# Scaling gathered rows on ScalarE and one 18-row product for the masked maximum in a four-layer graph network on one core

## The chip, the core and the metric

One NeuronCore of a Trainium2 chip runs the whole program. It has TensorE (PE, with its weight loads listed as PEld), VectorE (DVE), ScalarE (ACT), GpSimd (POOL) and SyncE (SP), each with its own in-order instruction queue, joined by semaphores. The metric is the device time of one execution in microseconds, as the median of several runs.

## What is computed

Four graph layers over 6,250 nodes and 106,250 edges with 128 features; each adds its result to x. Only layer 0 is touched. It is a hypergraph attention layer applied twice (l = 0, 1):

```
xt = x @ W;  et = he_attr @ W
a = leaky_relu(xt[row] @ att[:H] + et[col] @ att[H:], 0.2)
amax = segment_max(a, col);  ex = exp(a - amax[col]);  den = segment_sum(ex, col)
eout = segment_sum((Binv[col] * w * ex / den[col])[:, None] * xt[row], col)
nout = segment_sum((Dinv[row] * w * ex / den[col])[:, None] * eout[col], row)
x = tanh(layernorm(nout + bias) + x)
```

The other three layers are an edge perceptron with a segment sum, a gated message layer, and two graph attentions with four heads.

## The kernel before, in words

The kernel sorts the edges twice (by destination and by source, into blocks of 128 nodes), and then makes eight passes over the sorted edges, `ORDER = "abafcdee"`. A pass handles 512 edge slots, four tiles of 128, at a time; that is a group, and a pass of layer 0 has 232. Layer 0 has four passes. The first and third are of kind `a` (by destination: masked running maximum, exponentials, sum into the destination blocks). The second is `b` and the fourth `f` (by source: the same attention weights read back, and the sum into the source blocks).

For each group POOL issues four indirect DMAs (`rows_po`, line 615) that gather 128 rows of 132 floats of the node table. DVE compares slot numbers with an iota and so makes one-hot tiles (`aOH`, `bOH`, 128x512). PE transposes them, spreads per-node numbers to edge slots with them (L883, L942), and sums the scaled rows with them (L868, L921: four fp32 products of 128x130 or 128x129 columns). The maximum in `a` is made so: ACT turns the one-hot into 0 or -1e30 (L833), adds each row's score to it (L839, four times), PE transposes that (L876), and DVE reduces along the row (L740). The gathered rows are scaled by their weight in one DVE operation of 128x512 (L799 in `a`, L974 in `b`, L1061 in `f`), which writes `aR` or `bR`, the moving operand of the sum.

All loops are software pipelines written out by hand: `sweep` calls `body(j)` on every engine, and inside it `turn(j, u, lag)` picks the group j - lag. What an engine does in iteration j is in the order of the text, and a wait holds back everything behind it on that engine. So two things count: the lag of each step and its place inside the iteration. In `b`, `b_pe(j)` does the sum of group j-5 first, then the bit product L668 and the spread of j-2, then the transposes L934 of j-1. `b_ac(j)` copies the transposed one-hot of j-1 (L1007), takes the exponential of j-3 (L1012) and copies the bits of j-2 (L672). In `f`, `f_pe(j)` does the bit product of j-2, the transposes of j-1, the sum of j-4 and the spread of j-1. The gathered tile ring `aG` has 8 entries, `bG` 4: POOL may start the gathers of group g when semaphore `S.r` says that the rows of g-8 (in `b` and `f` g-4) are scaled. `l0_ve` builds the table of a layer before its `a` pass, 13 items of four blocks, and `meet` is a barrier of all engines.

## Time and profile before

| | us |
|---|---|
| median of 3 runs | 14665.91 (14642.43 to 14757.12) |
| span of the profiled execution, first to last instruction | 11822.6 |
| difference of the two | 2843.3 |
| DVE, PE, POOL busy in the span | 8126.2, 8182.0, 7702.8 |
| layer 0: passes a, b, a, f | from 1015 to 2252, 2273 to 3508, 3604 to 4839, 4861 to 6085 |

The page of the profile gives the shares over the whole span. The passes have different limits, so they are read one by one in windows of the trace. A period below is the time that one group takes, a pass divided by 232.

### The profile page before, as it was taken

How to read it: one execution, taken by the hardware profiler on the slowest of the kernel's cores; microseconds unless marked ns; L12 is line 12 of the kernel's file. 1: busy time of each engine (PE TensorE's matmuls, PEld its weight loads, DVE VectorE, ACT ScalarE, POOL GpSimd, SP SyncE). 2: the span in 40 equal slices, each digit the busy share in tenths (PEclk: the TensorE clock that was granted, in tenths of full speed). 3: DMA queues.
4: the chain of work that ended last, by engine and by line, in shares of the span. 5: the costliest groups of instructions: out<-in, count | busy, mean ns of one | idle time of the engine just before them, and what ended most of it. 6: DMA issues, size and time to landing. Idle time of an engine off the chain costs nothing. (4 is left out here: it accounts for less than half of the span.)

```text
span 11822.6 us, 182142 instructions
## 1 busy us (share of the span) xinstructions
PE 8182.0 (69%) x47949; PEld 6566.7 (56%) x47949; DVE 8126.2 (69%) x31101; ACT 5076.1 (43%) x14757; POOL 7702.8 (65%) x7673
## 2 busy tenths in 40 slices
PE   7895777666656777555545555788886677767776
PEld 5675777544436777444434554666665444545554
DVE  9765888655556777655562222688887788878888
ACT  4553444322224444222231111466665566646665
POOL 2445777677766777677757777355653677747775
PEclk8876666655556667666567677899998666556566
DMA  1112222355542222578844444344443444434443
GB/s 17 9 20 55 53 53 53 74 130 130 128 110 60 53 53 53 134 203 205 205 131 130 132 131 128 101 145 146 147 146 100 132 134 134 133 105 134 133 134 114
DMA packets 712736, 1297.08 MB, mean 110 GB/s; under 512 B 196563, under 2 KB 369073, under 8 KB 711217
## 3 DMA queue, kind: packets, MB, share of 16 engines
q0 software_dynamic: 282368, 575.57, 22.4%
q1 hardware_dynamic: 388992, 615.05, 16.6%
q10 hardware_dynamic: 40368, 94.82, 2.1%
q8 instruction: 415, 6.80, 0.2%
q14 instruction: 593, 4.85, 0.1%
HBM read 1050.01 MB, written 234.74 MB: 109 GB/s over the span
## 5 line engine op out<-in xcount | busy, mean ns | idle before, releaser
L615 POOL DMA_INDIRECT WK<-tab,IDX x4640 | 4624.3, 997 | 1688.7 <-issue 1345.2
L1454 POOL DMA_INDIRECT B<-tab,IDX x1856 | 1774.7, 956 | 848.5 <-issue 507.3
L615 POOL DMA_INDIRECT H<-tab,IDX x928 | 878.9, 947 | 644.1 <-DVE H L1260 346.4
L1473 DVE TENSOR_REDUCE WK<-PS 128x4 f32<-128x1024 f32 x928 | 1130.4, 1219 | 190.9 <-PE PS L1599 188.6
L1584 ACT ACTIVATE B<-B 128x33 f32<-128x33 f32 x5568 | 1211.2, 308 | 8.0
L839 ACT ACTIVATE WK<-WK 128x128 f32<-128x128 f32 x1856 | 592.6, 390 | 1289.5 <-DMA WK<-tab,IDX 1265.9
L921 PE MATMUL PS<-WK 128*128 128x129 f32 x3712 | 744.2, 362 | 429.6 <-DVE WK L974 208.8
L1632 PEld LDWEIGHTS PS<-B,H 128*128 128x128 f32 x3712 | 819.8, 330 | 283.0 <-issue 274.3
L1632 PE MATMUL PS<-B,H 128*128 128x132 f32 x3712 | 880.7, 430 | 87.3 <-DVE ACC L1486 87.3
L921 PEld LDWEIGHTS PS<-WK 128*128 128x128 f32 x3712 | 638.3, 259 | 527.1 <-DVE WK L974 268.0
L921 PE MATMUL PS<-WK,B 128*128 128x129 f32 x3712 | 829.1, 394 | 12.1 <-ACT WK L1160 8.5
L1599 PE MATMUL PS<-B 27*128 27x512 bf16 x1856 | 736.8, 509 | 138.4 <-DVE WK L1473 134.3
L868 PE MATMUL PS<-B 128*128 128x130 f32 x3712 | 802.7, 385 | 1.6 <-DVE B L799 1.6
L921 PEld LDWEIGHTS PS<-WK,B 128*128 128x128 f32 x3712 | 748.9, 298 | 14.0 <-issue 13.1
L1144 DVE TENSOR_TENSOR WK<-PS,WK 128x512 f32<-128x512 f32 x232 | 160.4, 691 | 850.7 <-DMA WK<-tab,IDX 850.7
L455 POOL DMA_INDIRECT pieces<-WK,B x208 | 354.5, 1704 | 571.6 <-ACT WK L443 308.3
L868 PEld LDWEIGHTS PS<-B 128*128 128x128 f32 x3712 | 715.7, 286 | 2.2 <-DVE B L799 2.2
L883 PEld LDWEIGHTS PS<-WK,B 128*128 128x128 f32 x3712 | 655.8, 264 | 70.3 <-issue 68.5
L883 PE MATMUL PS<-WK,B 128*128 128x2 f32 x3712 | 624.5, 290 | 45.1 <-DVE WK L796 43.3
L1192 PE MATMUL PS<-B 128*128 x2784 | 307.8, 273 | 500.9 <-DVE WK L1144 491.8
L861 PE MATMUL PS<-WT,B 128*128 128x128 bf16 x1856 | 233.1, 266 | 604.7 <-ACT B L844 520.6
L1160 ACT ACTIVATE WK<-WK 128x512 f32<-128x512 f32 x232 | 146.7, 632 | 1028.2 <-DVE WK L1144 1028.2
(426 smaller groups left out, 19037.9 us busy)
## 6 DMA issues: line engine op xcount, KB each, us to landing
H<-onehots SPq DMA_DIRECT2D x232, 768.0 KB
B<-onehots SPq DMA_DIRECT2D x232, 384.0 KB
onehots<-B ACTq DMA_DIRECT2D x232, 384.0 KB
WK<-tab,IDX POOLq DMA_INDIRECT x4640
onehots<-WK SPq DMA_DIRECT2D x232, 256.0 KB
B<-onehots SPq DMA_DIRECT2D x232, 256.0 KB
WK<-onehots SPq DMA_DIRECT2D x232, 256.0 KB
onehots<-B SPq DMA_DIRECT2D x232, 128.0 KB
```

Of the source, the lines that this page charges most:

```text
L455: po.indirect_dma_start(out=recd[o], out_offset=bass.IndirectOffsetOnAxis(ap=ROWI[:, o, 2 * k + q:2 * k + q + 1], axis=0), in_=OUT[x % 4][ ...
L615: po.indirect_dma_start(out=G[:, g % n, k, :], out_offset=None, in_=table, in_offset=bass.IndirectOffsetOnAxis(ap=IDX[:, idx, t:t + 1], ax ...
L839: i = ac.activation(aXR[:, r % 4, k, :], aN1[:, 128 * k:128 * k + 128], ACT.Identity, bias=aG[:, r, k, 128:129])
L868: mm = pe.matmul(aAG(r, k // 2), aOH[:, r, k, :], aR[:, r % 2, k, 0:130], start=k % 2 == 0, stop=k % 2 == 1)
L883: mm = pe.matmul(as2[:, k, :], aOT[:, r % 4, 128 * k:128 * k + 128], aY[:, r % 2, k // 2, 1:3], start=True, stop=True)
L921: mm = pe.matmul(AG(r, k // 2), OH[:, r, k, :], R[:, r % n, k, 0:129], start=k % 2 == 0, stop=k % 2 == 1)
L1192: mm = pe.matmul(PS[:, r % 4, 128 * k:128 * k + 128], cSTt[r % 4][:, 128 * k:128 * k + 128], SQP[:, bass.ds(v[k // 2] * 384 + 128 * i, 128 ...
L1454: po.indirect_dma_start(out=eG[:, g % 4, k, :], out_offset=None, in_=tab[TW3], in_offset=bass.IndirectOffsetOnAxis(ap=IDX[:, o, t:t + 1], ...
L1473: ve.tensor_reduce(eM2[:, g, b:b + 2, 2 * i:2 * i + 2, 1] if isinstance(g, int) else eM2[:, bass.ds(g, 1), b:b + 2, 2 * i:2 * i + 2, 1].re ...
L1584: i = ac.activation(eR[:, q, k, 33 * h:33 * h + 33], eG[:, r, k, 33 * h:33 * h + 33], ACT.Copy, scale=eEX[:, r, 4 * k + h:4 * k + h + 1])
L1599: mm = pe.matmul(PS[:, b + h, :], eSEL[:, b + h, :], eET[:, r, 512 * i:512 * i + 512], start=True, stop=True)
L1632: mm = pe.matmul(eAG(k // 2), eSTo[:, r, k // 4, 128 * (k % 4):128 * (k % 4) + 128], eR[:, r % 2, k, 0:132], start=k % 2 == 0, stop=k % 2 ...
```

## The change

The scaling of gathered rows moves from DVE (one 128x512 operation) to ACT (four 128x128 operations with the weight as per-row scale): in `a_ac` at lag 7, and for `b` and `f` in a new `rows_ac`, at the end of the ACT iteration, lag 4 and 3. In `a`, column 128 of `aR` is now made by a second exponential on ACT, and column 129 only in layer l = 0.

The masked maximum of `a` is made without L833, L839 and L876. PE multiplies seven bits of the transposed one-hot (`BITA`, 18 rows, rows 0 to 2 zero) and adds into rows 0 to 2 the score as three bf16 parts, which stand in the table's columns 260 to 262 counted in bf16. ACT copies the 18x512 result with a scale and bias that complement the bits, and PE multiplies it with an 18-row matrix (`SELA`) that gives score minus 1e30 for each bit that differs. `BITA` and `SELA` are made once (`pick_pe`). The spread to edge slots takes three bf16 parts in place of fp32 (`aSTm`), and DVE adds the parts up (`tensor_reduce` into `aS2`). DVE splits the new maximum in bf16 parts (four small operations), copies six columns of the per-block state at a time, and does the one-hot later in the iteration, behind a wait for the sum of group j-8. The lags of `a` grow by one. `l0_ve` writes the bf16 parts of the score in the table and in the state.

```
-                m, e, x, f, w = turn(j, u, 3), turn(j, u, 5), turn(j, u, 8), turn(j, u, 0), turn(j, u, 6)
+                m, e, x, f, w = turn(j, u, 4), turn(j, u, 6), turn(j, u, 9), turn(j, u, 0), turn(j, u, 7)
...
-                    ve.tensor_tensor(aE, aG[:, re_, :, 128], as2[:, :, 0], ALU.add).then_inc(S.e1, 1)
+                    ve.tensor_reduce(aS2.rearrange("p k c -> p (k c)"), as2.rearrange("p k c s -> p (k c) s"), AX.X,
+                                     ALU.add).then_inc(S.sv, 1)
...
-                    mx = aSF[:, bass.ds(vm[0] * 2 + 1, 1)]
-                    ve.tensor_copy(aOLD[:, 0, 0:1], mx)
-                    ve.tensor_copy(aY[:, qm, 0, 1:2], aSF[:, bass.ds(vm[0] * 2, 1)])
-                    ve.tensor_tensor(mx, mx, aTM[:, 0:1], ALU.max).then_inc(S.m1, 1)
+                    ve.wait_ge(S.ns, at.ns + gm)
+                    ve.wait_ge(S.s2, at.s2 + gm - 1)
+                    ve.wait_ge(S.mx, at.mx + gm)
+                    ve.tensor_copy(aST[:, qm, 0, 0:6], aSF[:, bass.ds(vm[0] * 6, 6)]).then_inc(S.m1, 1)
...
                     ve.wait_ge(S.ex, at.ex + gw + 1)
+                    ve.wait_ge(S.ag, at.ag + gw - 1)
+                    if l == 0:
+                        ve.scalar_tensor_tensor(aR[:, qw, :, 129], we, -1.0, we, ALU.mult, ALU.max)
                     ve.tensor_tensor(aEW[:, qw, :], aEX[:, rw, 0:4], we, ALU.mult).then_inc(S.p3, 1)
-                    ve.tensor_copy(aR[:, qw, :, 128], aEX[:, rw, 0:4])
-                    ve.scalar_tensor_tensor(aR[:, qw, :, 129], we, -1.0, we, ALU.mult, ALU.max)
...
+                    ve.tensor_copy(aST[:, qm, 1, 0:6], aSF[:, bass.ds(vm[1] * 6, 6)]).then_inc(S.sb, 1)
...
-                if w:
-                    ve.wait_ge(S.p3, at.p3 + gw + 1)
-                    ve.tensor_tensor(aR[:, qw, :, 0:128], aG[:, rw, :, 0:128],
-                                     aEW[:, qw, :].unsqueeze(2).broadcast_to([128, 4, 128]), ALU.mult).then_inc(S.r, 1)
...
+                if f:
+                    gf, rf = f
+                    ve.wait_ge(S.ag, at.ag + gf - 7)
+                    ve.tensor_tensor(aOH[:, rf, :, :], io4, low(0, gf), ALU.is_equal).then_inc(S.oh, 1)
...
-                    ve.scalar_tensor_tensor(aY[:, qm, :, 2], aT2[:, :, 1], 0.2, aT2[:, :, 1], ALU.mult,
-                                            ALU.max).then_inc(S.ns, 1)
-                    ve.scalar_tensor_tensor(aY[:, qm, :, 0], aT2[:, :, 0], 0.2, aT2[:, :, 0], ALU.mult,
-                                            ALU.max).then_inc(S.m6, 1)
+                    ve.scalar_tensor_tensor(aL, aT2, 0.2, aT2, ALU.mult, ALU.max).then_inc(S.m6, 1)
...
+                    ve.tensor_copy(aSTb[:, qm, :, 4], aL[:, :, 1]).then_inc(S.z, 1)
+                    ve.tensor_tensor(aDD[:, rm, 4:6], aL[:, :, 0], aL[:, :, 1], ALU.subtract).then_inc(S.m5, 1)
+                    ve.wait_ge(S.z, at.z + gm + 1)
+                    ve.tensor_tensor(aD1, aL[:, :, 1], aSTb[:, qm, :, 4], ALU.subtract).then_inc(S.gp, 1)
+                    ve.wait_ge(S.gp, at.gp + gm + 1)
+                    ve.tensor_copy(aSTb[:, qm, :, 5], aD1).then_inc(S.gl, 1)
+                    ve.wait_ge(S.gl, at.gl + gm + 1)
+                    ve.tensor_tensor(aSTb[:, qm, :, 6], aD1, aSTb[:, qm, :, 5], ALU.subtract).then_inc(S.ns, 1)
...
         def a_ac(ac, p):
             at, ring = raised_before(p)
@@ -828,28 +869,31 @@
             def body(j, u):
                 if f := turn(j, u, 1):
                     g, r = f
-                    ac.wait_ge(S.oh, at.oh + g + 1)
-                    ac.wait_ge(S.xr, at.xr + g)
-                    ac.activation(aN1, aOH[:, r, :, :].rearrange("p k n -> p (k n)"), ACT.Identity, bias=aNB,
-                                  scale=BIG).then_inc(S.n1, 1)
-                    ac.wait_ge(s_ring[r], landed(g, r, 8, ring[r]))
-                    ac.wait_ge(S.xt, at.xt + g - 3)
-                    ac.wait_ge(S.n1, at.n1 + g + 1)
-                    for k in range(4):
-                        i = ac.activation(aXR[:, r % 4, k, :], aN1[:, 128 * k:128 * k + 128], ACT.Identity,
-                                          bias=aG[:, r, k, 128:129])
-                    i.then_inc(S.xr, 1)
                     ac.wait_ge(S.pt, at.pt + g + 1)
-                    ac.wait_ge(S.s2, at.s2 + g - 3)
-                    ac.activation(aOT[:, r % 4, :], PS[:, 4, 0:256].bitcast(BF16), ACT.Copy).then_inc(S.ot, 1)
-                if f := turn(j, u, 5):
+                    ac.wait_ge(S.s2, at.s2 + g - 7)
+                    ac.activation(aOTb[:, r, :], PS[:, 4, 0:256].bitcast(BF16), ACT.Copy).then_inc(S.ot, 1)
+                if f := turn(j, u, 2):
+                    g, r = f
+                    ac.wait_ge(S.xr, at.xr + g + 1)
+                    ac.wait_ge(S.xt, at.xt + g - 1)
+                    ac.activation(aETb[:, r % 2, :], PS[0:18, 2 + r % 2, :], ACT.Identity, bias=abi[0:18, :],
+                                  scale=asc[0:18, :]).then_inc(S.n1, 1)
+                if f := turn(j, u, 6):
                     g, r = f
                     ac.wait_ge(S.p2, at.p2 + g + 1)
                     ac.activation(aEX[:, r, :], aDD[:, r, :], ACT.Exp).then_inc(S.ex, 1)
+                if f := turn(j, u, 7):
+                    g, r = f
+                    ac.wait_ge(S.p3, at.p3 + g + 1)
+                    ac.wait_ge(S.ag, at.ag + g - 1)
+                    ac.activation(aR[:, r % 2, :, 128], aDD[:, r, 0:4], ACT.Exp)
+                    for k in range(4):
+                        i = ac.activation(aR[:, r % 2, k, 0:128], aG[:, r, k, 0:128], ACT.Copy, scale=aEW[:, r % 2, k:k + 1])
+                    i.then_inc(S.r, 1)
             meet(ac)
-            sweep(5, body)
-
...
+                if f := turn(j, u, 3):
+                    g, r = f
+                    pe.wait_ge(S.n1, at.n1 + g + 1)
+                    pe.wait_ge(S.tm, at.tm + g - 1)
+                    pe.matmul(PS[:, r % 2, :], SELA, aETb[:, r % 2, :], start=True, stop=True).then_inc(S.xt, 1)
+                if f := turn(j, u, 8):
                     g, r = f
                     pe.wait_ge(S.r, at.r + g + 1)
                     pe.wait_ge(S.xb, at.xb + g - 1)
+                    n = 129 if l else 130
                     for k in range(4):
-                        mm = pe.matmul(aAG(r, k // 2), aOH[:, r, k, :], aR[:, r % 2, k, 0:130], start=k % 2 == 0,
+                        mm = pe.matmul(aAG(r, k // 2)[:, 0:n], aOH[:, r, k, :], aR[:, r % 2, k, 0:n], start=k % 2 == 0,
                                        stop=k % 2 == 1)
                     mm.then_inc(S.ag, 1)
+                if f := turn(j, u, 5):
+                    g, r = f
+                    pe.wait_ge(S.ns, at.ns + g + 1)
+                    pe.wait_ge(S.sv, at.sv + g)
+                    for k in range(4):
+                        mm = pe.matmul(as2[:, k, :, :], aOTb[:, r, 128 * k:128 * k + 128],
+                                       aSTm[:, r % 2, k // 2, :, :], start=True, stop=True)
+                    mm.then_inc(S.s2, 1)
                 if f := turn(j, u, 2):
                     g, r = f
-                    pe.wait_ge(S.xr, at.xr + g + 1)
-                    pe.wait_ge(S.tm, at.tm + g - 1)
+                    pe.wait_ge(S.ot, at.ot + g + 1)
+                    pe.wait_ge(S.n1, at.n1 + g - 1)
+                    pe.matmul(PS[0:18, 2 + r % 2, :], BITA, aOTb[:, r, :], start=True, stop=False)
+                    pe.wait_ge(s_ring[r], landed(g, r, 8, ring[r]))
                     for k in range(4):
-                        t = pe.transpose(PS[:, r % 2, 128 * k:128 * k + 128], aXR[:, r % 4, k, :], ident[:, :])
-                    t.then_inc(S.xt, 1)
-                if f := turn(j, u, 4):
-                    g, r = f
-                    pe.wait_ge(S.ns, at.ns + g + 1)
-                    pe.wait_ge(S.e3, at.e3 + g)
-                    for k in range(4):
-                        mm = pe.matmul(as2[:, k, :], aOT[:, r % 4, 128 * k:128 * k + 128], aY[:, r % 2, k // 2, 1:3],
-                                       start=True, stop=True)
-                    mm.then_inc(S.s2, 1)
+                        t = pe.matmul(PS[0:3, 2 + r % 2, 128 * k:128 * k + 128], aGb[:, r, k, 260:263], identb, start=False,
+                                      stop=k == 3)
+                    t.then_inc(S.xr, 1)
             meet(pe)
-            sweep(7, body)
+            sweep(8, body)
...
+        def rows_ac(ac, at, g, r):
+
+            ac.wait_ge(S.p3, at.p3 + g + 1)
+            ac.wait_ge(S.ag, at.ag + g - 1)
+            for k in range(4):
+                i = ac.activation(bR[:, r % 2, k, 0:128], bG[:, r % 4, k, 0:128], ACT.Copy, scale=bEW[:, r % 2, k:k + 1])
+            i.then_inc(S.r, 1)
...
-                    ve.wait_ge(S.p3, at.p3 + g + 1)
-                    ve.tensor_tensor(bR[:, q, :, 0:128], bG[:, r % 4, :, 0:128],
-                                     bEW[:, q, :].unsqueeze(2).broadcast_to([128, 4, 128]), ALU.mult).then_inc(S.r, 1)
...
                 if f := turn(j, u, 2):
                     bits_ac(ac, 1, *f, bTBb, 6, 2)
-            sweep(3, body)
+                if f := turn(j, u, 4):
+                    rows_ac(ac, at, *f)
+            sweep(4, body)
 
...
                     ac.dma_start(oht[0][g], TB[r % 4]).then_inc(s_k0[r % 4], 16)
                     ac.dma_start(bitd[0][g], TBb[r % 4]).then_inc(s_k0[r % 4], 16)
-            sweep(2, body)
+                if f := turn(j, u, 3):
+                    rows_ac(ac, at, *f)
+            sweep(3, body)
 
...
+                own(ve, "ve", ve.tensor_copy(Tb[:, 0:n, 260], P[:, :, 128]))
                 ve.tensor_copy(TS0[t % 4][:, 0:n, 0:129], P)
+                own(ve, "ve", ve.tensor_tensor(TSD[:, 0:n], P[:, :, 128], Tb[:, 0:n, 260], ALU.subtract))
+                own(ve, "ve", ve.tensor_copy(Tb[:, 0:n, 261], TSD[:, 0:n]))
+                ve.tensor_tensor(Tb[:, 0:n, 262], TSD[:, 0:n], Tb[:, 0:n, 261], ALU.subtract)
...
+            own(ve, "ve", ve.memset(aSF, 0.0))
             ve.tensor_copy(SF[:, :, 0], NV[:, :, 4])
             ve.memset(SF[:, :, 1], -BIG)
+            split_ve(ve, lambda i: aSFb[:, :, i], NV[:, :, 4], S3)
...
+                if l == 0:
+                    pick_pe(pe)
```

## Rows read from the trace of the kernel before

**Rows 1.** Windows of passes a, b, f, c: us; PE, PEld, DVE, ACT, POOL; clock, DMA, GB/s
```profile
1015.00:2270.00 1255.00, 930.95 (x5568) 904.36 (x5568) 988.91 (x5817) 572.71 (x1624) 929.93 (x928) 0.68 0.23 53
2275.00:3512.00 1237.00, 776.32 (x3940) 549.17 (x3940) 643.53 (x2794) 338.92 (x696) 943.27 (x927) 0.52 0.54 128
...
4865.00:6092.00 1227.00, 675.60 (x3940) 528.22 (x3940) 651.18 (x2800) 311.27 (x695) 932.05 (x926) 0.62 0.78 203
6200.00:7395.00 1195.00, 676.36 (x4695) 598.22 (x4693) 299.18 (x735) 151.58 (x242) 882.65 (x928) 0.72 0.45 129
```

**Rows 2.** Groups of POOL instructions in the windows of a, b, f, c
```profile
L615 POOL DMA_INDIRECT WK<-tab,IDX x930 | 932.3, 1002 | 400.4 <-issue 258.1 <-SPq L148 73.0 <-DVEq L148 44.6
...
L615 POOL DMA_INDIRECT WK<-tab,IDX x927 | 943.5, 1018 | 282.5 <-issue 271.5 <-DVE WK L974 11.0
...
L615 POOL DMA_INDIRECT WK<-tab,IDX x926 | 932.6, 1007 | 282.3 <-issue 275.3 <-DVE WK L1061 7.0
...
L615 POOL DMA_INDIRECT WK<-tab,IDX x928 | 882.7, 951 | 340.9 <-issue 282.5 <-DVEq L148 58.4
```

**Rows 3.** Waits, longest first, in the windows of a and b
```profile
ACT WK L839 <- DMA WK<-tab,IDX: 636.7, 229, 6.3
...
PE PS L921 <- DVE WK L974: 208.8, 218, 3.6
```

**Rows 4.** Timeline in pass a: a DVE one-hot and the gather begun under it
```profile
1542.21 0.68 DVE L778 TENSOR_TENSOR B<-iof,LOW 128x512 f32<-128x512 f32 x1
1542.26 1.46 POOL L615 DMA_INDIRECT WK<-tab,IDX  x1 [0.30 <-issue]
```

**Rows 5.** Timeline in pass b, one group on PE and ACT
```profile
2700.97 0.20 ACT L1012 ACTIVATE WK<-WK 128x4 f32<-128x4 f32 x1 [3.17 <-DVE WK L992]
2701.08 0.76 ACT L672 ACTIVATE B<-PS,WT 15x512 bf16<-15x512 f32 x1
...
2701.62 0.61 PE L934 MATMUL PS<-WT,WK 128*128 128x128 bf16 x4 [0.80 <-DVE WK L915]
...
2702.32 0.60 ACT L1007 ACTIVATE B<-PS 128x512 bf16<-128x512 bf16 x1 [0.49 <-issue]
...
2703.12 2.09 PE L921 MATMUL PS<-WK 128*128 128x129 f32 x8 [0.89 <-DVE WK L974]
...
2705.14 0.60 PE L668 MATMUL PS<-B,WT 128*15 128x512 bf16 x1
...
2705.67 0.27 PE L942 MATMUL PS<-B 128*128 x4
```

**Rows 6.** Timeline in pass a: ACT and PE at the low clock
```profile
1503.75 1.28 ACT L839 ACTIVATE WK<-WK 128x128 f32<-128x128 f32 x4 [2.37 <-DMA WK<-tab,IDX]
...
1505.41 0.19 ACT L848 ACTIVATE WK<-WK 128x6 f32<-128x6 f32 x1
1505.51 0.71 ACT L833 ACTIVATE WK<-B,WK 128x512 f32<-128x512 f32 x1
...
1506.03 2.04 PE L868 MATMUL PS<-B 128*128 128x130 f32 x8
...
1507.87 1.06 PE L876 MATMUL PS<-ident,WK 128*128 128x128 f32 x4
```

**Rows 7.** Timeline in pass f: the sum at the high clock, an ACT DMA issue
```profile
5304.37 1.11 PE L921 MATMUL PS<-WK,B 128*128 128x129 f32 x8
...
5304.69 0.46 ACTq L1098 DMA_DIRECT2D bits<-B  x1
```

**Rows 8.** Groups by form, whole trace: ACT with scale and bias per row
```profile
L1347 ACT ACTIVATE WK<-X,WK 128x128 f32<-128x128 f32 x928 | 380.2, 486 | 8.0 <-DVE WK L1292 8.0
```

**Rows 9.** Timeline of `l0_ve`: two table items, one period apart
```profile
984.69 0.70 DVE L1759 COPY WK<-PS 128x516 f32<-128x516 f32 x1 [0.56 <-PE PS L1662]
...
986.02 0.70 DVE L1759 COPY WK<-PS 128x516 f32<-128x516 f32 x1 [0.56 <-PE PS L1662]
```

More of the change, by code:

```diff
@@ L138, in build @@
         bti = WT[:, 1376:1383].bitcast(I32)
+        SELA = PICK[0:18, 0:64].bitcast(BF16)
+        BITA = PICK[:, 64:73].bitcast(BF16)
+        asc, abi = PICK[:, 73:74], PICK[:, 74:75]
         pidi = WT[:, 1383:1384].bitcast(I32)
@@ L662, in bits_ve, with pick_pe @@
             own(ve, "ve", ve.tensor_scalar(bsc, bbi, -2.0, 1.0, ALU.mult, ALU.add))
+            own(ve, "ve", ve.memset(BITA[:, 0:3], 0.0))
+            ve.tensor_copy(BITA[:, 3:18], BITS[:, 0:15])
+            own(ve, "ve", ve.tensor_scalar(abi, pidx, 10.0, None, ALU.is_ge))
+            ve.tensor_scalar(asc, abi, -2.0, 1.0, ALU.mult, ALU.add)
+            ve.memset(pick[:, 0:3], 1.0)
+            ve.tensor_scalar(pick[:, 3:10], bti, BIG, -BIG, ALU.mult, ALU.add)
+            ve.tensor_scalar(pick[:, 10:17], bti, -BIG, None, ALU.mult)
+            ve.memset(pick[:, 17:18], -BIG).then_inc(s_pick, 1)
+            ve.wait_ge(s_pick, 2)
+            own(ve, "ve", ve.tensor_copy(SELA, PS[0:18, 6, 0:64].bitcast(BF16)))
+        def pick_pe(pe):
+            pe.wait_ge(s_pick, 1)
+            pe.transpose(PS[0:18, 6, 0:64].bitcast(BF16), pick[:, 0:18], identb).then_inc(s_pick, 1)
         def bits_pe(pe, o, g, r, OT, bank, n):
@@ L1675, in build @@
         TS0 = [WK[:, 2048 + 4 * TW * i:2048 + 4 * TW * (i + 1)].rearrange("p (b c) -> p b c", c=TW) for i in range(4)]
+        TS0b = [WK[:, 2048 + 4 * TW * i:2048 + 4 * TW * (i + 1)].bitcast(BF16).rearrange("p (b c) -> p b c", c=2 * TW) for i in range(4)]
+        TSD = WK[:, 4200:4204]
         s_w0, s_rf, s_rfc = sem("w0"), sem("rf"), sem("rf_clear")
@@ L2475, in _ @@
                 l0_pe(pe, l)
+                if l == 0:
+                    pick_pe(pe)
                 meet(pe)
-                a_pe(pe, 2 * l)
+                a_pe(pe, 2 * l, l)
                 meet(pe)
```

73 lines of the change are left out of this document (41 added, 32 removed).

## Prediction

> **What bounds the kernel now.** I read the windows of the single passes first, then the groups and waits inside them, then the timeline of a few groups. The windows [rows 1] have no engine full: in a pass of kind a PE is busy 931 of 1255 us, DVE 989, ACT 573, POOL 930. The groups of POOL [rows 2] show why POOL sets the pace all the same. Between two gathers stands about 0.30 us of issue that is not counted as busy. With the barrier waits left out (73.0 and 44.6 in a, 58.4 in c) a gather costs (932.3 + 400.4 - 117.6) / 930 = 1.307 us in a, (943.5 + 282.5) / 927 = 1.323 in b, 1.312 in f and 1.255 in c. Four gathers are a group: 5.23, 5.29, 5.25 and 5.02 us. These are the periods of the passes, and nothing holds POOL but its own queue. The waits [rows 3] say the same from the other side: in a, ACT waits 636.7 us for gathered rows, 229 times in 232 groups.
>
> Two things in these rows matter. First, a gather takes 951 ns in c, but 1002, 1018 and 1007 in a, b and f [rows 2]. The timeline [rows 4] shows where it comes from: a gather that starts while DVE runs a 128x512 operation on two SBUF inputs takes 1.46 us. The excess is 51 x 928 = 47 us in a pass a, 62 in b, 52 in f. There are two such operations in each group (the one-hot and the row scale), so a half of it belongs to the one that goes. The Trainium skill (SBUF — State Buffer, Who interferes with whom) has this as a rule: a DVE operation with two SBUF inputs contends with a GpSimd instruction that reads SBUF. By that rule the excess of the scale goes and the small two-input operations that are added count a little against it; the trace agrees as far as that the stretched gather began under the operation.
>
> Second, the gathers take 11.8 ms of trace, and the median is 2843 us above the span. I add changes to the median as if this part stayed.
>
> **What goes and comes on each engine.** On DVE 0.68 us of row scale per group goes in all four passes. In a, DVE ran 5817 / 232 = 25 operations a group and by the new text again 25: four copies become two, one exponent copy goes, and a sum of parts and four splitting operations come. So DVE has about 989 - 158 = 830 us of work in a pass a, and is no bound. The gain there is only that POOL is disturbed less.
>
> On ACT the four scales cost what four additions with a per-row operand cost, 1.28 us in a row [rows 6]. With scale and bias per row it was 486 ns each [rows 8], against 390; that is the upper end, 0.4 us more. In b and f ACT was busy 339 and 311 us [rows 1], so it has room for 1.28 x 232 = 297 us. Busy time is not the question; the question is behind what ACT does it.
>
> **Pass b turns into a ring.** In iteration j of `b_pe` the sum of group j-5 comes first and waits for `S.r` of j-5. That is now raised by the last step of ACT's iteration j-1. All of PE's iteration is queued behind this wait, with the transposes of j-1 last. ACT's iteration j begins with the copy L1007, which waits for those transposes, and everything of ACT, the new scales last, is queued behind it. So PE's and ACT's iterations no longer overlap: one turn is one group. Before, `S.r` came from DVE (PE waited for it 218 times, 208.8 us [rows 3]), and no such ring closed. Its length by [rows 5], at the low clock that holds in b (granted 0.52 [rows 1]):
> PE: sum to the next product 2705.14 - 2703.12 = 2.02; bit product to spread 0.53; spread 0.27; transposes 0.61: 3.43.
> ACT: an operation starts 0.1 before the former ends (L848 and L833 in [rows 6]), so copy 0.50, exponential 0.11, bits 0.66, four scales 1.28: 2.55.
> Two hand-overs, 0.09 (2701.62 + 0.61 to 2702.32) and about 0.1: 0.2.
> Sum 6.18 us, against 5.29 now. At the high clock the sum takes 1.11 in place of 2.04 [rows 6, 7]; PE's part shrinks to 1.85 and the ring to 4.6, below POOL's 5.02. The clock: PE's work will stand in one unbroken piece of 3.4 us, as it does in f, where 0.62 was granted, so somewhat more of it may run high than now. But a high stretch comes after the piece that earned it, and will fall in part on ACT's turn. I let 15% of PE's part run high: 3.43 x 0.15 x 0.46 = 0.24, period 5.95, 232 x 5.95 - 1227 = **+153 us**. Ends: POOL's pace with half the excess, 5.15 (-32 us), and 6.18 with the dearer scale, 6.6 (+300).
>
> **Pass f has no such ring.** `f_pe` does the transposes before the sum, and ACT's copy of them waits for nothing of the same round. The shortest ring through the scales (scales, sum 2.04, spread 0.27, the DVE chain about 1.2, exponential, copy, bits, 0.8 of DMA issues [rows 7], scales) is about 7.5 us over two groups. ACT gets 311 / 232 + 0.8 + 1.28 = 3.4 us of work, under 5.02. The scales end some 4 us after the gathered rows of the next group land, and the ring of four lets that come 10 us after: POOL doesn't wait. So f keeps POOL's pace and loses a half of its excess: **-26 us** (ends -52 and 0).
>
> **Pass a, twice.** ACT loses 0.71 (L833) and 1.28 (L839), and gets 0.76 (18x512, as L672 [rows 5]), a small exponential and 1.28. PE loses the fp32 transposes (1.06) and fp32 spreads, and gets two bf16 products of 512 columns and four of 128. Here too a ring closes: ACT's copy of 18x512 waits for the last step of `a_pe(j-1)`, the scales come behind it on ACT, and the sum in `a_pe(j)` waits for them, with the spread, `BITA` and the four score products behind it. Its length at the low clock: ACT 0.66 + 0.1 + 0.1 + 1.28 = 2.14; PE 1507.87 - 1506.03 = 1.84 for the sum, 0.27 for the spread, 0.53 and 0.6 for the products as in [rows 5]: 3.24; hand-overs 0.2. Sum 5.58. At the high clock 2.14 + 1.75 + 0.2 = 4.1. Granted were 0.68 in a, so 36% of the time high; with that the ring takes 5.58 - 3.24 x 0.36 x 0.46 = 5.04. That is POOL's own pace, 5.02 to 5.12. Of two limits so close each waits for the other at times; I take 5.30, +0.07, **+16 us** for each pass, 32 for both. Ends: 5.12 (-25 each) and 5.58 (+81 each). The Trainium skill (TensorE: Matmul & The Clock Gate, HAM oscillation — how this bites in real kernels) speaks against the change: bursts of matmuls with waits between them let the clock fall. By that rule a would end at its low-clock ring, which is the second case below.
>
> **Between the passes.** `l0_ve` has a period of 1.33 us [rows 9], set by PE and ACT, and DVE's 0.85 in it becomes about 1.6 with four small operations that wait for each other: 0.27 x 13 = 4 us per layer, 1 for the splitting of 49 columns, and 2 once for `SELA`: **+12 us** (5 to 25).
>
> **Sum:** 153 - 26 + 32 + 12 = +171. 14665.91 + 171 = **14837 us**; the span should go from 11822.6 to about 11994.
>
> **The other ways it could go.**
> (1) The forecast, b's ring at the low clock, a near POOL's pace: chance 0.45, 14837, its own range 14740 to 14920.
> (2) The clock falls in a too, since PE waits there more and works less, and a runs at 5.58: 2 x 81 + 153 - 26 + 12 = +301, 14967. For it: the granted clock in b is 0.52 with the same kind of gaps. Against: at the low clock PE would still be busy 4.4 of 5.6 us. Chance 0.22.
> (3) Not slower: POOL stays the bound in b as well, because the ring is shorter than 5.15 there. This decides itself at 2.6 us of PE's part in place of 3.43, that is if half of PE's work in b ran at the high clock. Then b gives -32, a -25 twice, f -26, the rest +12: -96, 14570. Against it: 0.52 granted. Chance 0.13.
> (4) The change does little to the time that is measured: the 2843 us that the profile doesn't show lie in the gathers. Eight passes of 928 gathers [rows 2] are 7424; with 2843 / 7424 = 0.38 us more each POOL's pace in layer 0 would be 4 x 1.63 = 6.5 us, and b's ring would hide behind it; left would be some of the excess: -40 or so, 14620. For it: the difference is large and I know no place for it. Chance 0.12.
> The rest, 0.08, is for what I have not seen, mostly on the slow side.
>
> **Range and chances.** 1% (147 us) is about what a measurement of this kernel can tell from no change. Slower by over 1% is above 14813: 0.6 of case 1, all of case 2, most of the rest: 0.54. Faster by over 1% is below 14519: 0.05. Within 1%: 0.41. The range runs from 14600, inside cases 3 and 4, to 15040, which is case 2 with b near its upper end: 0.8.
>
> **What the profile after would show.** b: a window of about 1380 us for its 232 groups, POOL waiting for ACT's scales, ACT waiting for PE's transposes L934 and PE's sum waiting for ACT nearly every time. a: periods of 5.1 to 5.6, with ACT's 18x512 copy waiting for PE; f: 5.1 to 5.2 and gathers of about 980 ns. Wrong would be the forecast if b's period is under 5.3 (then the ring isn't closed, or the clock is high), if f got a ring too, or if the span moved and the median didn't.

## The result, and the profile after

| | before, us | after, us | ratio, 95% interval |
|---|---|---|---|
| where the shown times were taken | 14654.17 (4 runs) | 14975.38 (4 runs) | 1.022 [1.019, 1.025] |
| a second time in that condition (`e4_after_again`) | 14679.75 (11) | 14966.05 (5) | 1.0194 [1.0167, 1.022] |
| in the other condition (`e12_after_usual`) | 11835.39 (8) | 11877.32 (5) | 1.0036 [1.0022, 1.005] |

The change costs 2% or a third of a per cent, and this has to be said before anything else, since no number below can be understood without it: the kernel before takes 14.65 ms in one condition and 11.83 ms in another (11839, 11829, 11835 and 11835 us on three chips, 14680 on a fourth). The span of 11822.6 us shown of before is from the second, and the median 14665.91 beside it from the first. I call them the long and the short condition and compare only inside one. Whether the condition belongs to the chip or to something that passes is not shown: the record has one chip with the long one, in one job.

The profiled execution of after is from the long condition, its time 14940.97 us, its span 14939.2. Its passes, in the columns of [rows 1] (stretch, length, busy time of PE, PEld, DVE, ACT, POOL, granted clock, DMA, GB/s; a, b, a, f, c):

```profile
1020.00:2648.00 1628.00, 916.23 (x5003) 620.14 (x5003) 931.63 (x5661) 604.18 (x1805) 888.60 (x928) 0.59 0.17 39
2701.00:4175.00 1474.00, 716.50 (x3907) 503.39 (x3907) 522.12 (x2529) 576.87 (x1605) 882.48 (x928) 0.55 0.44 107
4290.00:5904.00 1614.00, 915.80 (x5003) 615.88 (x5003) 899.60 (x4990) 591.32 (x1805) 877.52 (x928) 0.59 0.17 40
5957.00:7582.00 1625.00, 755.12 (x3915) 555.02 (x3915) 503.73 (x2528) 598.76 (x1607) 890.43 (x928) 0.53 0.58 153
7731.00:9116.00 1385.00, 714.29 (x4506) 575.06 (x4507) 268.06 (x667) 142.23 (x225) 882.34 (x928) 0.64 0.37 108
```

Set against [rows 1] every pass is longer, c by 190 us, and nobody touched c. POOL is busy the same time; it is its waiting that grew. So these rows can't be subtracted from those of before. The rows that can are those of the same changed kernel in the short condition (`e12_after_usual`, its profiled run 11866.51 us; windows of a, b, a, f, then POOL's group in each):

```profile
1030.00:2226.00 1196.00, 852.00 (x5031) 567.15 (x5032) 927.29 (x5717) 596.25 (x1820) 912.55 (x928) 0.64 0.24 54
2269.00:3594.00 1325.00, 709.20 (x3908) 495.62 (x3909) 526.25 (x2534) 578.84 (x1610) 883.72 (x928) 0.57 0.50 119
3706.00:4889.00 1183.00, 835.68 (x5026) 554.42 (x5026) 898.01 (x5033) 595.79 (x1819) 899.83 (x928) 0.66 0.24 54
4932.00:6116.00 1184.00, 748.48 (x3920) 547.99 (x3920) 496.16 (x2539) 602.25 (x1611) 896.78 (x928) 0.54 0.85 211
```
```profile
L619 POOL DMA_INDIRECT WK<-tab,IDX x928 | 912.5, 983 | 359.9 <-issue 276.1 <-SPq L152 77.4 <-ACT B L891 6.4
...
L619 POOL DMA_INDIRECT WK<-tab,IDX x928 | 883.7, 952 | 483.8 <-ACT WK L1011 223.0 <-issue 217.0 <-DVEq L152 43.9
...
L619 POOL DMA_INDIRECT WK<-tab,IDX x928 | 899.9, 970 | 344.0 <-issue 273.7 <-SPq L152 61.5 <-ACT B L891 8.8
...
L619 POOL DMA_INDIRECT WK<-tab,IDX x928 | 896.9, 966 | 329.3 <-issue 281.2 <-DVEq L152 43.6 <-ACT WK L1011 4.5
```

Before against after, pass by pass, from the first gather to the end of the last (before from `e1_before_again`; a period is the distance of gathers four apart, mean over the pass):

| pass | before, us | period | after, us | period | difference |
|---|---|---|---|---|---|
| a | 1209 | 5.21 | 1195 | 5.15 | -14 |
| b | 1231 | 5.31 | 1324 | 5.71 | +92 |
| a | 1198 | 5.16 | 1182 | 5.10 | -15 |
| f | 1214 | 5.23 | 1183 | 5.10 | -31 |
| c | 1165 | 5.02 | 1165 | 5.02 | 0 |

All of the loss is in b, and there POOL waits 223.0 us for ACT's line L1011, the row scales; in [rows 2] it waited 11.0 us for anything in b. In a and f it still waits for nothing of weight, and its gathers are shorter (983 and 966 ns against 1002 and 1007 [rows 2]). Of the stretches between the passes, the one from b to the second a grows from 104 to 113 us and the one from f to c from 143 to 147; the start of the first a lies anywhere from 1016 to 1041 us, with either kernel.

### The profile page after: what moved, and what is told of

It is laid out like the page before. It is cut to its first block and busy times, and to the rows that moved or that the text cites. A ratio compares the mean times of both kernels' runs of the same rounds, so it can differ in the third digit from the quotient of the medians.

```text
span 14939.2 us, 184357 instructions
## 1 busy us (share of the span) xinstructions
PE 8386.0 (56%) x47022; PEld 6071.2 (41%) x47022; DVE 7842.6 (52%) x30526; ACT 5694.6 (38%) x17077; POOL 7504.9 (50%) x7673
## 3 DMA queue, kind: packets, MB, share of 16 engines
q14 instruction: 621, 5.09, 0.1%
## 5 line engine op out<-in xcount | busy, mean ns | idle before, releaser
L619 POOL DMA_INDIRECT WK<-tab,IDX x4640 | 4423.0, 953 | 3610.6 <-issue 1466.4
L879 ACT ACTIVATE B<-PS,PICK 18x512 bf16<-18x512 f32 x464 | 357.0, 769 | 1947.8 <-remote 1299.0
L918 PE MATMUL PS<-B,WK 128*128 128x130 f32 (+1 forms) x3712 | 898.2, 417 | 328.2 <-issue 178.0
L961 DVE TENSOR_TENSOR ACC<-ACC,PS 128x129 f32 x928 | 263.9, 284 | 1452.8 <-remote 662.7
L918 PEld LDWEIGHTS PS<-B,WK 128*128 128x128 f32 x3712 | 768.4, 306 | 543.8 <-issue 272.3
L974 PEld LDWEIGHTS PS<-WK,B 128*128 128x128 f32 x3712 | 761.9, 295 | 527.1 <-issue 280.6
L847 DVE TENSOR_TENSOR WK<-iof,LOW 128x512 f32<-128x512 f32 x464 | 320.3, 691 | 1108.6 <-remote 787.2
L1632 ACT ACTIVATE B<-PS 12x1024 bf16<-12x1024 bf16 x232 | 234.8, 1012 | 1512.0 <-remote 764.9
L1658 PEld LDWEIGHTS PS<-B 27*128 27x128 bf16 x1856 | 132.5, 102 | 1480.1 <-issue 728.0
L905 PE MATMUL PS<-WT,WK 128*128 128x128 bf16 x1856 | 271.4, 298 | 781.4 <-DVE WK L847 762.2
L1011 ACT ACTIVATE WK<-WK 128x128 f32<-128x128 f32 x1856 | 588.7, 388 | 243.2 <-issue 94.4
```

Of the source, the lines that this page charges most:

```text
L619: po.indirect_dma_start(out=G[:, g % n, k, :], out_offset=None, in_=table, in_offset=bass.IndirectOffsetOnAxis(ap=IDX[:, idx, t:t + 1], ax ...
L847: ve.tensor_tensor(aOH[:, rf, :, :], io4, low(0, gf), ALU.is_equal).then_inc(S.oh, 1)
L879: ac.activation(aETb[:, r % 2, :], PS[0:18, 2 + r % 2, :], ACT.Identity, bias=abi[0:18, :], scale=asc[0:18, :]).then_inc(S.n1, 1)
L918: mm = pe.matmul(aAG(r, k // 2)[:, 0:n], aOH[:, r, k, :], aR[:, r % 2, k, 0:n], start=k % 2 == 0, stop=k % 2 == 1)
L974: mm = pe.matmul(AG(r, k // 2), OH[:, r, k, :], R[:, r % n, k, 0:129], start=k % 2 == 0, stop=k % 2 == 1)
L1011: i = ac.activation(bR[:, r % 2, k, 0:128], bG[:, r % 4, k, 0:128], ACT.Copy, scale=bEW[:, r % 2, k:k + 1])
```

## The experiments

All edits are to the kernel before or to the changed one; nothing is left out of the computation in any of them, and two add work whose result nobody reads.

**The kernel before once more, and the two halves of the change.** First the unchanged kernel, to learn what the 2843 us are.

> The kernel before, unchanged, profiled once more. The trace on which the prediction rests has a span of 11822.6 us beside a median of 14666; the profile of the changed kernel has 14939 beside 14975. Theory A: the first trace is of an execution without some stops that all the timed ones have; then the new span is about 14600 us, and the passes c, d and e, which nothing touches, have periods of about 7.0, 6.7 and 7.5 to 8.8 us as in the changed kernel, and not 5.0, 6.2 and 5.3 (per 512 slots). Theory B: the stops came with the change; then the span is about 11820 us again and c has 5.0 us.

Measured: 11826.96 us, span 11825.1. The time is the span and 1.9 us. There is nothing outside the profile. The number is the one theory B gives; what stands behind it was seen with the later runs: this one and the median are of different conditions.

In `e2_only_a` DVE keeps the row scale of b and f:

```
 # b_ve, f_ve, behind S.p3; rows_ac and its two calls are gone
+ve.tensor_tensor(bR[:, q, :, 0:128], bG[:, r % 4, :, 0:128],
+                 bEW[:, q, :].unsqueeze(2).broadcast_to([128, 4, 128]), ALU.mult).then_inc(S.r, 1)
```

> Only the two passes a are changed (masked maximum by an 18-row product, bf16 parts, row scale on ScalarE); in b and f the row scale is on VectorE as before. The prediction's sum gives +32 for a and +12 between the passes: +44 us, ratio 1.003. Rival: a pays most of the 321 us (its ring at the low clock, 5.4 to 5.6 us): ratio 1.015 or more.

Measured: 11807.67 against 11839.15 us, 0.997 [0.996, 0.998]. In `e3_only_bf` pass a is as before and `rows_ac` is in b and f:

```
-ve.tensor_tensor(bR[:, q, :, 0:128], bG[:, r % 4, :, 0:128],
-                 bEW[:, q, :].unsqueeze(2).broadcast_to([128, 4, 128]), ALU.mult).then_inc(S.r, 1)
+if f := turn(j, u, 4):          # b_ac; in f_ac lag 3
+    rows_ac(ac, at, *f)
```

> Only the row scale of b and f is moved to ScalarE; a is as before. The prediction's sum gives +153 in b (PE and ACT in one ring) and -26 in f: +127 us, ratio 1.009. Rival that a pays: ratio 1.000 to 1.005. If the two parts add up, the ratios of this run and of the run with only a together make the 1.022 of the whole change.

Measured: 11912.94 us, 1.0058 [1.0042, 1.0075]. POOL's group in a of the first and in b of the second (L958 is the row scale there):

```profile
L619 POOL DMA_INDIRECT WK<-tab,IDX x928 | 912.2, 983 | 366.7 <-issue 275.7 <-SPq L152 84.0 <-ACT B L891 7.0
```
```profile
L615 POOL DMA_INDIRECT WK<-tab,IDX x928 | 884.3, 953 | 483.6 <-ACT WK L958 221.7 <-issue 217.0 <-DVEq L148 44.8
```

Both rows are those of the whole change, within 1 ns of a gather. So a's part is worth -31 us, b's and f's together +74, and these stand in the passes where they were made.

**The whole change in both conditions.**

> The changed kernel as it is, beside the two runs that each held one half of the change (only a: 11808 us, 0.997 of before; only b and f: 11913 us, 1.006 of before). Theory 1, the parts add up: every pass is bound on its own, so the whole is 11839 - 31 + 74 = 11880 us, a ratio of 1.003, pass b at 5.7 us per group, a at 5.15, f at 5.10. Theory 2, the parts interact (ScalarE or the clock of TensorE carries something from one pass to the next): the whole is at 1.02 as in the first measurement, 12080 us, with a above 5.4.

Measured in the long condition: 14966.05 against 14679.75 us, 1.0194. There theory 2 has its number but not its reason, since c, d and e are longer too. A second profiled execution of the same kernel lies in the short condition, with a span of 11867.5 us: theory 1's number.

> The changed kernel once more, in a job whose runs of the kernel before should lie at 11830 us and not at 14680 (as they did beside the last run of this kernel). Theory 1, the parts add up: 11840 - 31 + 74 = 11880 us, a ratio of 1.003, with a at 5.15, b at 5.70 and f at 5.10 us per group. Theory 2, the change costs 2 per cent here too, since a, b and f together load ScalarE more than each half: 12070 us. If before lies at 14680 again, the ratio is 1.02 once more.

Measured in the short condition: 11877.32 against 11835.39 us, 1.0036 [1.0022, 1.005]. The parts (-31 and +74) add up to the whole (+42) within 1 us, with the periods that theory 1 gave: 5.15, 5.71, 5.10. ScalarE carries nothing from one pass into another.

**The ring in b.** What binds b can be seen in two groups of the changed kernel in the short condition (timeline; start, length, engine and line; the idle time before it in brackets):

```profile
2904.59 2.09 PE L974 MATMUL PS<-WK 128*128 128x129 f32 x8 [2.65 <-ACT WK L1011]
2904.81 0.95 POOL L619 DMA_INDIRECT WK<-tab,IDX  x1 [1.19 <-ACT WK L1011]
...
2906.61 0.60 PE L690 MATMUL PS<-B,WT 128*15 128x512 bf16 x1
...
2907.14 0.27 PE L995 MATMUL PS<-B 128*128 x4
...
2907.27 0.59 PE L987 MATMUL PS<-WT,WK 128*128 128x128 bf16 x4
...
2907.94 0.60 ACT L1065 ACTIVATE B<-PS 128x512 bf16<-128x512 bf16 x1 [3.40 <-issue]
2908.44 0.20 ACT L1070 ACTIVATE WK<-WK 128x4 f32<-128x4 f32 x1
2908.53 0.76 ACT L694 ACTIVATE B<-PS,WT 15x512 bf16<-15x512 f32 x1
...
2909.20 1.26 ACT L1011 ACTIVATE WK<-WK 128x128 f32<-128x128 f32 x4
...
2910.51 2.09 PE L974 MATMUL PS<-WK 128*128 128x129 f32 x8 [2.65 <-ACT WK L1011]
```

While PE works (2904.59 to 2907.86) ACT stands, 3.40 us; while ACT works (2907.94 to 2910.46) PE stands, 2.65. One turn is 5.92 us. The long condition has the same turn to 0.01 us where nothing else disturbs it (3399.78 to 3405.70 there). If this is a ring by the order of TensorE's text, then another order opens it:

```
 # b_pe, one iteration
+turn(j - 1)                     # the transposes, moved up from the end
 bits(j - 2)
-sum(j - 5)                      # was first
+sum(j - 5)
 spread(j - 2)
-turn(j - 1)
```

> The changed kernel, with one edit: in pass b TensorE issues the transposes of group j-1 first in an iteration, then the bits product, then the sums of group j-5, then the spread, where it had the sums first and the transposes last. Theory 1, the ring through TensorE and ScalarE bounds b: the ring is cut, POOL sets the pace again, b falls from 5.7 to 5.1 us per group (as f, whose order this is), its gathers stay near 960 ns, POOL's wait before L619 in b falls from 150 us to under 20, and the time falls by 130 us to about 11750. Theory 2, the pace of b is set by how much ScalarE or TensorE has to do in an iteration and not by their order: b stays at 5.6 to 5.7 and the time at 11880. Theory 3, the order only moves the wait to VectorE: b at 5.4 and 11810.

This one was measured in the long condition and came out at 15050.89 us, 1.0254 [1.0227, 1.028] of before, slower than the changed kernel's 1.0194; b went from 6.32 to 6.67 us per group. None of the three theories says that. A second profiled execution of it is of the short condition, span 11714.1 us against 11867.5 of the changed kernel. Its windows of the first a and of b, and POOL's group in b:

```profile
1026.00:2218.00 1192.00, 855.93 (x5027) 568.25 (x5027) 927.43 (x5713) 595.89 (x1820) 909.36 (x928) 0.63 0.23 54
2263.00:3444.00 1181.00, 753.42 (x3920) 560.27 (x3920) 480.90 (x2539) 580.30 (x1615) 898.46 (x928) 0.52 0.57 134
...
L619 POOL DMA_INDIRECT WK<-tab,IDX x928 | 898.5, 968 | 327.1 <-issue 266.4 <-DVEq L152 44.6 <-ACT WK L1011 16.1
```

There b takes 5.09 us per group, POOL's wait for L1011 is 16.1 us, and a stays as it was (5.14 and 5.11): the one edit does what theory 1 says, where nothing else disturbs it. With a's order changed as well:

```
 # a_pe, one iteration
 turn(j - 1);  SELA(j - 3)
+BITA and the four score products (j - 2)
 sum(j - 8);  spread(j - 5)
-BITA and the four score products (j - 2)
```

> The kernel of the run before with one more edit: in pass a TensorE issues the product with BITA and the four products of the scores before the sums of group j-8, where they stood last in the iteration. Theory 1 (POOL's four gathers bound a in any order, the ring of a is hidden): a stays at 5.15 us per group in both passes and the time at 11750. Theory 2 (the ring of a costs something in stretches of the low clock): a falls by 0.05 to 0.10 us per group, 12 to 23 us in each of two passes, and the time to 11710 to 11730.

Measured, long condition: 15012.41 us, 1.0224 [1.0195, 1.0254]; a fell from 7.02 to 6.92. In a second profiled execution, short condition, span 11676.3 us, a fell from 5.14 and 5.11 (`e5_b_turn_first`) to 5.06 and 5.02. That is the size that theory 2 gave, but not its reason, as POOL had waited only 7.3 us for ACT in a whole pass. Then the same kernel in the short condition:

> The changed kernel with both orders of TensorE changed (in b the transposes first and the sums third; in a the product with BITA and the scores' products before the sums). Where before took 14680 us this cost in b (6.32 to 6.65 us per group) and gained in a (7.02 to 6.92), but there TensorE stood still in stretches and POOL was not the bound. Theory 1, the ring of b through ScalarE's scaling and TensorE's sums bounds b when TensorE runs evenly: b falls from 5.70 to 5.1 us per group with gathers near 960 ns, a stays at 5.15, and the time is 11740 to 11760 us, 0.993 of before. Theory 2, ScalarE's and VectorE's own chain of a group (exponent, scaling, p3) sets b's pace in any order: b stays at 5.6 to 5.7 and the time at 11870. Theory 3, the new order costs in b as it did before: b at 5.9 or above, 11930 us.

Measured: 11692.86 against 11835.39 us, 0.9877 [0.986, 0.9893]. It beats both kernels, and theory 1 by 50 us. POOL's groups in a and b, and their windows:

```profile
L619 POOL DMA_INDIRECT WK<-tab,IDX x928 | 885.9, 955 | 365.9 <-issue 263.6 <-SPq L152 83.4 <-ACT B L891 18.9
...
L619 POOL DMA_INDIRECT WK<-tab,IDX x928 | 901.5, 971 | 327.6 <-issue 266.4 <-DVEq L152 45.0 <-ACT WK L1011 16.2
```
```profile
1029.00:2198.00 1169.00, 938.04 (x5027) 625.66 (x5027) 925.79 (x5693) 641.71 (x1820) 885.94 (x928) 0.56 0.25 55
...
2243.00:3427.00 1184.00, 752.16 (x3921) 558.97 (x3922) 481.47 (x2539) 580.43 (x1615) 901.18 (x928) 0.52 0.59 134
```

b is 140 us shorter (5.71 to 5.11 per group), POOL's wait for L1011 went from 223.0 to 16.2 us, and PE and ACT have the operations they had. The order alone did it; theories 2 and 3 fall. The 50 us more are in a: 5.15 to 5.04 and 5.10 to 5.02. POOL had waited for nothing there before either; its gathers went from 983 to 955 ns. The engine that became quicker is the same, POOL; what the order of TensorE changed is when DVE's one-hot (L847, which waits for the sum of group j-8) falls against the gathers. Counted over the first pass a, 130 of 928 gathers started under L847 with the old order and 24 with the new one; what the gathers take above 951 ns each fell from 30 to 3 us in all. The pair of runs that differ by a's order alone says the same: 125 gathers in `e5_b_turn_first`, 34 in `e6_ab_order`. And a's granted clock fell, from 0.64 to 0.56, while the pass became shorter: it had PE as no bound.

Then the ring made on purpose, in f:

```
 # f_pe, one iteration
-bits(j - 2);  turn k_pe(j - 1);  sum(j - 4);  spread(j - 1)
+sum(j - 4);  bits(j - 2);  spread(j - 1);  turn k_pe(j - 1)
```

> The changed kernel, with one edit in pass f: TensorE issues the sums of group j-4 first and the transposes of k_pe last, the order of pass b. Theory 1 (the ring comes from the order): f rises from 5.10 us per group to 5.5 to 5.8, POOL waits 90 to 160 us before L619 in f, and the time rises by 90 to 160 us over the changed kernel, to about 12000. Theory 2 (ScalarE's or TensorE's work sets the pace, not its order): f stays at 5.10 and the time at 11880.

In the long condition: 14952.31 us, 1.018 [1.0148, 1.0212], f at 6.95 us per group against 7.03. That told nothing apart, as the ring would hide behind such a pace. In the short one:

> The changed kernel with pass b's order of TensorE put into pass f: the sums of group j-4 first, the transposes of k_pe last. In the last job turning b's order the other way took b from 5.71 to 5.11 us per group. Theory 1 (the order makes the ring): f, now 5.10 us per group with POOL waiting 3 us, rises to 5.6 to 5.9 and POOL waits 120 to 180 us in it; the time rises from 11877 to 12000 to 12060 us where before takes 11835. Theory 2 (b's ring needs something that f has not, for instance that ScalarE's copy in b also waits for the spread): f stays at 5.10 to 5.20 and the time below 11900. If before lies at 14680, f stays near 7.0, as in the first run of this kernel, and nothing is told apart.

Measured: 12301.98 against 11834.61 us, 1.0391 [1.0374, 1.0408]; f rose from 5.10 to 6.91 us per group, 420 us for the pass. POOL's group, the waits of PE's sum and of ACT's copy of the transposes (in 5000 to 6500 us), and one turn:

```profile
L619 POOL DMA_INDIRECT WK<-tab,IDX x928 | 904.6, 975 | 742.0 <-ACT WK L1011 482.7 <-issue 215.9 <-DVEq L152 43.4
```
```profile
PE PS L974 <- ACT WK L1011: 797.7, 215, 4.2
ACT B L712 <- PE PS L706: 712.5, 215, 3.3
```
```profile
5504.63 2.09 PE L974 MATMUL PS<-WK,B 128*128 128x129 f32 x8 [3.62 <-ACT WK L1011]
...
5507.99 0.60 ACT L712 ACTIVATE B<-PS 128x512 bf16<-128x512 bf16 x1 [3.32 <-PE PS L706]
...
5509.27 0.33 ACTq L1154 DMA_DIRECT2D onehots<-B  x1
5509.62 0.64 ACTq L1155 DMA_DIRECT2D bits<-B  x1
5510.36 1.28 ACT L1011 ACTIVATE WK<-WK 128x128 f32<-128x128 f32 x4 [1.12 <-issue]
...
5511.69 2.09 PE L974 MATMUL PS<-WK,B 128*128 128x129 f32 x8 [3.80 <-ACT WK L1011]
```

The turn is 7.06 us. Theory 1 is right in kind and 1.1 us too low in size: it took b's turn for f and forgot that f's ACT issues two DMAs in front of the scales, 5509.27 to 5510.36, which now stand in the ring.

**What stretches a gather.** Pass c has no DVE operation on two SBUF operands and gathers of 951 ns. One was added per group:

```
 # c_ve, ahead of the addition into cZ
+ve.tensor_tensor(cX[:, r % 2, :].rearrange("p (k n) -> p k n", n=128), io4, low(0, g), ALU.is_equal)
```

> The kernel before with one VectorE operation more per group in pass c, ahead of the addition into cZ: a comparison of io4 with the low parts, 128x512 in fp32, two operands in SBUF, written to a buffer that nobody reads (the form of the one-hot operation of the other passes). Pass c has no such operation, and its gathers took 951 ns at 5.02 us per group. Theory 1 (a gather that starts under such an operation is stretched): the mean gather of c rises to 980 to 1010 ns and the pass by 0.12 to 0.24 us per group, 28 to 56 us in all; single gathers reach 1.4 us. Theory 2 (the stretched gathers of the other passes come from their wider rows or from other transfers): c stays at 951 ns and 5.02 us.

And in its place one with a single SBUF operand, `ve.tensor_scalar(cX..., io4, 64.0, None, ALU.is_equal)`:

> The same place and size with one operand in SBUF: a comparison of io4 with a constant, 128x512 in fp32. Theory 1a (it is the second SBUF operand that stands in the gather's way): c stays at 951 to 955 ns and 5.02 us per group. Theory 1b (any VectorE operation of this length that reads only SBUF does it): the gathers rise as with two operands, to 980 to 1010 ns.

Measured in c: gathers of 960 and 956 ns, 5.058 and 5.041 us per group, against 951 ns and 5.024 in `e1_before_again`; 11845.83 and 11862.7 us against 11829.21, single executions that tell nothing at this size. Rows of POOL and of the added operation, with two operands and then with one:

```profile
L615 POOL DMA_INDIRECT WK<-tab,IDX x871 | 835.9, 960 | 265.5 <-issue 265.5
L1145 DVE TENSOR_TENSOR WK<-iof,LOW 128x512 f32<-128x512 f32 x218 | 151.7, 696 | 682.8 <-DMA WK<-tab,IDX 682.8
```
```profile
L615 POOL DMA_INDIRECT WK<-tab,IDX x874 | 834.8, 955 | 266.4 <-issue 266.4
L1145 DVE TENSOR_SCALAR WK<-iof 128x512 f32<-128x512 f32 x219 | 99.2, 453 | 735.4 <-DMA WK<-tab,IDX 735.4
```

The mechanism is there, with a third of the least size that was expected (9 ns where 29 to 59 were). Single gathers show it:

```profile
6792.90 0.69 DVE L1145 TENSOR_TENSOR WK<-iof,LOW 128x512 f32<-128x512 f32 x1 [4.04 <-DMA WK<-tab,IDX]
6792.95 1.47 POOL L615 DMA_INDIRECT WK<-tab,IDX  x1 [0.30 <-issue]
```
```profile
6284.24 0.43 DVE L1145 TENSOR_SCALAR WK<-iof 128x512 f32<-128x512 f32 x1 [2.55 <-DMA WK<-tab,IDX]
6284.28 1.20 POOL L615 DMA_INDIRECT WK<-tab,IDX  x1 [0.31 <-issue]
```

In both a gather begun under the operation ends about 0.82 us after the operation's end (6794.42 - 6793.59; 6285.48 - 6284.67), and so it does in [rows 4] (1543.72 - 1542.89). So it is held at its start until DVE is done, and pays only for what is left of the operation then. All gathers of a pass bear it out: in the first a of the trace of before, 161 of 928 gathers start under L778 or L799, the two operations with two SBUF operands, and these hold 45 of the 47 us that the gathers take above 951 ns each. The 140 that start under L740, a reduction of 128x512 out of PSUM, take 0.96 us at most, and so do the 106 that start in c of `e1_before_again` under L1144, an addition of 128x512 with one operand in PSUM. In c the added operation starts when a gather's rows have landed, and only 76 gathers start under it, 30 of them held (46 and 17 with one operand). Of theories 1a and 1b the second has the right kind, though not its size: one SBUF operand is enough in this form, which takes 453 ns where the other takes 696. That any operation on SBUF alone would do it is not shown. The Trainium skill (SBUF — State Buffer, Who interferes with whom) has both cases: two SBUF inputs, and scalar operations in a faster mode that takes the shared port pair. The trace agrees, the 453 ns being the sign of that mode.

## Why the prediction was right, and where it was not

The forecast was 14837 us, +171, slower with chance 0.54. The measured pair in the long condition is +321, inside the range; in the short condition it is +42, which is "within 1%". The side was right where it was measured first, but not by my sum: that was made from rows of the short condition, and there it is four times too large (the span is 11864.8, where 11994 was forecast). That the side and the range fit in the long condition is in good part luck: 42 of the 286 us that `e4_after_again` shows are the cost seen in the short condition, and where the other 244 arise the runs do not show.

- **What bounds the kernel:** right for the rows it rests on. POOL's four gathers set the pace of a, b, f and c. In the long condition it is not so: POOL waits 461.6 us in the first pass a of the changed kernel and 222.2 us in c.
- **"I add changes to the median as if this part stayed."** This is the step that failed. The 2843 us were no fixed part outside the layer's passes. The changed kernel pays 432, 149, 431 and 441 us for the long condition in a, b, a and f (1628 - 1196, and so on, by the windows above), 219 in c. How before pays there, pass by pass, no trace here shows; from the times alone its whole is 2844 where the changed one's is 3089.
- **Pass b, +153:** measured +92. The ring is there, with the engines and lines that the prediction named, and it opens and closes with the order. Its turn at the low clock was 6.18 in the sum and is 5.92: PE's part 3.27 and not 3.43, because the transposes begin 0.13 us after the spread and not 0.27; ACT's 2.52 and not 2.55; the two hand-overs 0.13 and not 0.2. The share at the high clock was put at 15% of PE's part; the mean of 5.71 is 0.21 under the turn, 0.21 / (3.27 x 0.46) = 14%. Of the 229 turns that the trace shows 174 take 5.9 us and the others 4.6 to 5.4. So the guess held and the parts were each a little high. 0.24 us too much in 232 groups is 56 of the 61 us.
- **Pass f, -26:** measured -31, POOL's pace, gathers of 966 ns.
- **Pass a, +16 each:** measured -14 and -15. The length of its ring was worked out as 5.04 on average, below POOL's 5.15, and then 5.30 was taken because "of two limits so close each waits for the other". They don't, in a ring with eight groups of room: POOL waits 6.4 us for ACT in the whole pass. With this the term would have been its lower end, -25; the gathers gave half of that, 15 ns (998 to 983) and not 25. The ring costs something all the same, as the new order shows, but by another way: it moves DVE's one-hot under the gathers.
- **DVE in a, 830 us:** it was 927, from 963 in the same stretch of `e1_before_again`. The row scale went, 158 us, and the small operations of the new tail gave back 122 of it. It bounds nothing, so nothing came of the error.
- **Half the excess of the gathers goes in every pass:** in b nearly all of it went (1023 to 952 ns) while POOL waits there; with the ring open, in `e5_b_turn_first`, the gathers of b take 968 ns. In f it went from 1003 to 966, in a from 998 to 983. A share by count of operations was no good measure; the phase decides. In `e1_before_again` the gathers that start under the row scale hold 20 of 43 us of excess in the first a, 41 of 66 in b and 34 of 55 in f; in f just these went, in a the one-hot's part rose meanwhile from 24 to 30.
- **Between the passes, +12:** +13 between them, but only some 3 of it from `l0_ve`. With only a changed (`e2_only_a`) the stretch ahead of the second a grows by 3 us; with only b and f changed (`e3_only_bf`), where `l0_ve` is as before, those behind b and f grow by 7 and 3. What comes before the first pass is not resolved, as its start differs by up to 25 us from run to run.
- **The rivals:** (2), the clock falls in a and a runs at 5.58: the granted clock did fall, 0.68 to 0.64, and with the other order to 0.56, with a at 5.04, but not to its low level, 0.5; what the clock does to PE's part is hidden while POOL is the bound. With the rule of the Trainium skill cited there (TensorE: Matmul & The Clock Gate, HAM oscillation), that waits between bursts of matmuls let the clock fall, the trace agrees in the direction alone, and not with the time that the rival made of it. (3), POOL stays the bound in b: no, 5.71. Its condition was also worked out wrong: for a ring under 5.15 PE's part would have to be 5.15 - 2.55 - 0.2 = 2.4 us and not 2.6, two thirds at the high clock and not half. (4), the missing 2843 us lie in the gathers: no, the gathers take 946 to 960 ns in the long condition too, and what grew is POOL's waiting. Its half-truth is that b's ring is nearly hidden there, 6.32 us with a stop now and then against 5.71.

## What to carry to other kernels

When work moves to another engine, look where the step that raises its semaphore stands in that engine's iteration, and what stands first in the iteration of the engine that waits for it: last on one and first on the other makes a ring of one group. Moving the waiting step back in its text was worth 140 us of 1324 here in the short condition, though in the long one it cost 0.33 us per group, so measure it in both. Where a median and a profiled span are far apart, run the unchanged kernel again before adding anything to either: they may be of two conditions. Of an engine whose waits are already zero, its operations may still become shorter by what another engine does at the time.
